# A selective scan and a routed feed-forward on one Trainium2 core: who makes the ten products du*B in the first half of each batch

## The reference, cut to what matters

```
delta = softplus(dt_proj @ dt_lo + bias)            # [b, e, t]
dA    = exp(delta * A[e, n])
state = state * dA + (delta * u)[e, t] * B[n, t]    # du*B: the product
y     = sum over n of state * C[n, t]
x     = x + transpose((y + D*u) * silu(layernorm(x)))
```

```
logits = layernorm(x).reshape(-1) @ switch_w.T + switch_b   # one routing per batch, top 2 of 8
h  = gelu(x_head @ w1[expert] + b1[expert])                 # 16 heads of 64
o  = sum over the two experts of gate * (h @ w2[expert] + b2[expert])
out = x + (layernorm(x) + o) @ w3.T + b3
```

## Time and profile before

| | |
|---|---|
| time, median of 3 | 2447.03 us |
| profiled execution | 2449.12 us, its span 2447.1 us |
| VectorE busy | 2121.5 us, 87% |
| TensorE busy | 1991.9 us, 81% |
| ScalarE busy | 1601.4 us, 65% |
| GpSimd busy | 1525.9 us, 62% |
| mean granted TensorE clock | 0.904 |

### The profile page before, as it was taken

The page is one execution under the profiler, slowest core; times in us unless marked ns, Lnnn a source line. Parts: engine busy times, 40 slices in busy tenths (PEclk is TensorE's granted clock), DMA queues, the critical chain, the costliest instruction groups (busy, mean ns, idle before and its releaser), DMA issues.

```text
span 2447.1 us, 32499 instructions
## 1 busy us (share of the span) xinstructions
PE 1991.9 (81%) x10584; PEld 1180.8 (48%) x10584; DVE 2121.5 (87%) x2694; ACT 1601.4 (65%) x2357; POOL 1525.9 (62%) x1061
## 2 busy tenths in 40 slices
PE   6898889986857987996757897898785787787899
PEld 2677667754533553443434454354453354344344
DVE  5899799979998999989999899998999899899311
ACT  2687877766668868655658977855666857854500
POOL 0698677767755765666766675576775577577111
PEclk9899999997878999997878998899786899899899
DMA  5311515555512944566621554466461174467512
GB/s 176 126 40 58 194 53 172 185 196 200 196 52 70 318 146 130 164 208 206 235 84 69 201 201 141 149 223 207 166 221 31 52 254 164 141 213 284 205 57 72
DMA packets 199290, 383.00 MB, mean 157 GB/s; under 512 B 30513, under 2 KB 96049, under 8 KB 199122
## 3 DMA queue, kind: packets, MB, share of 16 engines
q1 hardware_dynamic: 195952, 380.46, 46.2%
q10 hardware_dynamic: 3170, 0.47, 0.1%
HBM read 346.79 MB, written 34.08 MB: 156 GB/s over the span
## 4 chain that ended last, share of the span: by engine, by line
PE 32%; DVE 22%; issue 22%; ACT 16%; POOL 6%; DMA 1%; DVEq 1%; POOLq 0%; ACTq 0%; SPq 0%
DVE h L1547 10%; PE dense L1161 10%; PE dense L989 5%; POOL h L876 5%; ACT dA L1270 4%; DVE dense L1523 4%; PE dense L927 3%; ACT L1239 3%; PE dense L1086 2%; DVE u L1383 2%; PE dense L975 2%; PE dense L939 2%; PE dense L1144 2%; PE dense L996 2%; ACT hs L1357 2%
## 5 line engine op out<-in xcount | busy, mean ns | idle before, releaser
L876 POOL TENSOR_TENSOR h<-h,Cb 128x1024 f32<-128x1024 f32 x512 | 1208.3, 2361 | 375.0 <-DVE h L1547 349.1
L1270 ACT ACTIVATE dA<-delta,Av 128x512 f32<-128x512 f32 x1024 | 703.3, 716 | 390.9 <-DVE h L1547 387.9
L989 PE MATMUL dense<-ident,h 128*128 128x128 f32 x4096 | 601.6, 298 | 155.0 <-POOL h L876 154.3
L989 PEld LDWEIGHTS dense<-ident,h 128*128 128x128 f32 x4096 | 518.1, 155 | 309.7 <-POOL h L876 222.3
L1547 DVE TENSOR_TENSOR_SCAN h<-dA,state,dense 128x512 f32<-128x512 f32 x512 | 628.8, 1268 | 18.5 <-PE dense L989 7.6
L1547 DVE TENSOR_TENSOR_SCAN h<-dA,dense 128x512 f32<-128x512 f32 x512 | 597.2, 1205 | 12.9 <-PE dense L989 8.4
L1523 DVE TENSOR_TENSOR dense<-dense,Bb 128x512 f32<-128x512 f32 x864 | 552.4, 687 | 1.6
L1161 PE MATMUL dense<-w3h,xT 128*128 128x512 f32 x832 | 384.8, 598 | 1.3 <-DVE xT L1503 1.3
L870 POOL COPY state<-h 128x2 f32<-128x2 f32 x256 | 47.7, 186 | 319.3 <-DVE h L1547 317.6
L927 PE MATMUL dense<-ctxs,win 128*128 128x512 f32 x432 | 209.8, 631 | 10.2 <-ACT szT L1299 9.0
L1161 PEld LDWEIGHTS dense<-w3h,xT 128*128 128x128 f32 x832 | 148.3, 192 | 137.7 <-issue 135.8
(11 more groups left out here) (167 smaller groups left out, 2009.9 us busy)
## 6 DMA issues: line engine op xcount, KB each, us to landing
sww<-in_sw SPq DMA_DIRECT2D x167, 512.0 KB, 4.3
Cb<-bc_scratch SPq DMA_DIRECT2D x64, 512.0 KB, 6.6
Bb<-bc_scratch SPq DMA_DIRECT2D x54, 512.0 KB, 4.8
w3h<-in_sw SPq DMA_DIRECT2D x52, 512.0 KB, 8.0
w3h<-in_w3T SPq DMA_DIRECT2D x52, 512.0 KB, 5.2
row<-x_scratch SPq DMA_DIRECT2D x40, 512.0 KB, 4.8
xz<-in_x SPq DMA_DIRECT2D x64, 256.0 KB, 4.7
xt<-in_x SPq DMA_DIRECT2D x64, 256.0 KB, 4.1
```

The lines of the kernel that those rows point to most:

```text
L876: e.tensor_tensor(h[:, s:s + 2, :], h[:, s:s + 2, :], Cb[:, 2 * q:2 * q + 2, :], ALU.mult).then_inc(prod_done, 1)
L989: mm = e.matmul(yT[:, k, :], h[:, 2 * ((PAIRS * g + q) % RH) + i, k * P:(k + 1) * P], ident[:], is_transpose=True, start=False, stop=(q == ...
L1270: e.activation(dA[:, i % RA, :], delta[:, st % 2, :], ACT.Exp, scale=Av[:, j * N + n:j * N + n + 1]).then_inc(dA_done, 1)
```

## The change

TensorE makes the ten products in steps 0 to 7 of batches 1 to 3 too (`pe_step`: 24 more steps). With it:

- The product banks are laid out ahead by `ProductBanks`: F1, M0 and M1 in turn where TensorE makes products, M0 and M1 elsewhere, and the transposed du takes a turn in the same rotation instead of F0.
- F1 is therefore taken from the feed-forward in first halves: for `u=0` the second hidden half and the second tile bank are F2, `turn 0` uses F0 alone at its own, earlier slots, `turn 1` uses F1 and waits for the last scan of step 7; for `u=1` the tiles go F1, F0.
- `duT` has one buffer, copied in slot 7 behind the du copy. b3 gets half a buffer of its own (`b3half`), loaded four times a batch, each load waiting on SP for the addition before.
- The diagonals are no longer made from bank F2 by VectorE after batch 0's start: Bb is loaded for all pairs, and GpSimd masks it in place with `affine_select`, ten times at each of four chunk changes (into step 8 of batch 0 and step 0 of batches 1 to 3), four in the old chunk's last step and six in the new one's slots 0 to 3.

```diff
+HALF_PAIRS = PE_PAIRS
...
+def pe_step(g):
+    return g < STEPS or g % STEPS < J
...
 def on_pe(g, n):
-    return g < STEPS and n // 2 in PE_PAIRS
+    return pe_step(g) and n // 2 in (PE_PAIRS if g < STEPS else HALF_PAIRS)
-def product_bank(g, n):
-    return (F1, M0, M1)[(N * g + n) % 3] if g < STEPS else (M0, M1)[n % 2]
+class ProductBanks:
+    def __init__(self):
+        self.bank, self.before = {}, {}
+        order, held = [F1, M0, M1], {}
+        for g in range(ALL):
+            for n in range(N):
+                if n == N - 2 and g + 1 < ALL and pe_step(g + 1):
+                    self.place(order, held, ("turn", g + 1), order)
+                self.place(order, held, ("product", g, n), order if pe_step(g) else [k for k in order if k != F1])
...
+            for i in (0, 1):
+                t = ((11, 13), (17, 19), (24, 26), (27, 29))[k][i]
+                self.add(b, t, "turn", 0, k, i)
+                self.add(b, t + 1, "turned", 0, k, i)
...
+                self.add(b, at[W3C * (TB * dh - 1)] + 3 if dh else at[0] - 2, "b3_load", u, dh)
...
-            return [((what, *args), F0 + i if u == 0 or b == NB else F2)]
+            return [((what, *args), F0 + i if b == NB else F1 if u else F0)]
         if what == "hidden":
             first = M0 if b == NB and args[1] % 2 else F0
-            return [((what, *args, i), first + i) for i in (0, 1)]
+            second = F2 if b < NB and args[0] == 0 else first + 1
+            return [((what, *args, i), (first, second)[i]) for i in (0, 1)]
...
+            return [((what, *args[:3]), (F1, F0)[m % 2] if args[0] else (F0, F2)[m % 2])]
...
             def load_bc(c, q):
-                for i, dst in ((N, Cb),) if on_pe(J * c, 2 * q) else ((0, Bb), (N, Cb)):
+                for i, dst in ((N, Cb),) if c == 0 and on_pe(0, 2 * q) else ((0, Bb), (N, Cb)):
...
+            def diagonal_b(c, n):
+                e.wait_ge(bc_loaded[n // 2], bc_value(c, n // 2))
+                e.affine_select(out=Bb[:, n, :].rearrange("p (k t) -> p k t", k=TB), in_=Bb[:, n, :].rearrange("p (k t) -> p k t", k=TB),
+                                compare_op=ALU.is_equal, fill=0.0, base=0, pattern=[[0, TB], [-1, P]], channel_multiplier=1) \
+                    .then_inc(diag_done, 1)
...
+                    for n in range(N):
+                        at = n // 2 + 4 + n % 2
+                        if j == J - 1 and at == q and c + 1 < NB * TH and on_pe(g + 1, n):
+                            diagonal_b(c + 1, n)
+                        if j == 0 and at == SLOTS + q and c and on_pe(g, n):
+                            diagonal_b(c, n)
...
-                if b == 0:
-                    if q == 1 and j == J - 1 and g + 1 < STEPS:
-                        turn_b(c + 1, count(b, "x_proj", th) + 1)
-                    if q == 2:
-                        first_sum(g)
+                if b == 0 and q == 2:
+                    first_sum(g)
+                if b < NB:
                     times_b_at(N * g + 2 * q + 3)
-                    if q == SLOTS - 2 and g + 1 < STEPS:
-                        turn_du(g + 1)
+                    if q == SLOTS - 2 and g + 1 < ALL and pe_step(g + 1):
+                        if not pe_step(g):
+                            last = ("tile", 1, NQ - 1, TB - 2)
+                            e.wait_ge(evac[bank_of(b, *last)], 1 + count(b, *last) + 1)
+                        wait_product_bank(e, ("turn", g + 1))
+                        turn_du(g + 1, BANKS.bank[("turn", g + 1)])
...
                     if q == SLOTS - 1 and g + 1 < ALL:
                         copy_du(g + 1)
+                        if pe_step(g + 1):
+                            copy_duT(g + 1, BANKS.bank[("turn", g + 1)])
...
-                if j == J - 1 and g + 1 < STEPS and q and on_pe(g + 1, 2 * (q - 1)):
-                    for n in (2 * q - 2, 2 * q - 1):
-                        diagonal_b(c + 1, n)
```

More of the change, by code:

```diff
@@ L52, in conv_slot, with place @@
     return 2 if st % J == J - 1 else 1
+def pe_step(g):
+    return g < STEPS or g % STEPS < J
 def on_pe(g, n):
-    return g < STEPS and n // 2 in PE_PAIRS
-def product_bank(g, n):
-    return (F1, M0, M1)[(N * g + n) % 3] if g < STEPS else (M0, M1)[n % 2]
+    return pe_step(g) and n // 2 in (PE_PAIRS if g < STEPS else HALF_PAIRS)
[8 more added lines that the diff above has]
+                self.place(order, held, ("product", g, n), order if pe_step(g) else [k for k in order if k != F1])
+    def place(self, order, held, name, among):
+        k = among[0]
+        self.bank[name], self.before[name] = k, held.get(k)
+        held[k] = name
+        order.remove(k)
+        order.append(k)
+BANKS = ProductBanks()
 class Schedule:
@@ L222, in tail @@
         for dh in range(NQ):
+            self.add(b, 46, "b3_load", 0, dh)
+        for dh in range(NQ):
             for u in (0, 1):
@@ L320, in build @@
         du_s = sb("du_s", [P, T])
-        duT = sb("duT", [P, 2, TB, P])
+        duT = sb("duT", [P, TB, P])
+        b3half = sb("b3half", [P, QD])
         h = sb("h", [P, 2 * RH, T])
@@ L500, in chunk_block, with turns_of_du, diag_index, wait_product_bank @@
             return G // STEPS, G // J % TH, G % J
+        made = [0]
+        for g_ in range(ALL):
+            made.append(made[-1] + sum(on_pe(g_, m) for m in range(N)))
         def pe_index(g, n):
-            return 2 * len(PE_PAIRS) * min(g, STEPS) + sum(on_pe(g, m) for m in range(n))
+            return made[g] + (sum(on_pe(g, m) for m in range(n)) if g < ALL else 0)
         def vec_index(g, n):
             return N * g + n - pe_index(g, n)
-        def bank_free(g, n):
-            return N * g + n - (2 if g < STEPS else 1)
-        def bc_value(c, q):
-            return 1 + sum(16 if on_pe(J * i, 2 * q) else 32 for i in range(c + 1))
+        def turns_of_du(g):
+            return sum(pe_step(i) for i in range(g))
+        def diag_index(c, n):
+            return sum(on_pe(J * i, m) for i in range(c) for m in range(N)) + sum(on_pe(J * c, m) for m in range(n))
+        def wait_product_bank(e, name):
+            before = BANKS.before[name]
+            if before and before[0] == "product":
+                e.wait_ge(h_done, 1 + N * before[1] + before[2] + 1)
+            elif before:
+                e.wait_ge(duT_done, 1 + turns_of_du(before[1]) + 1)
+        def bc_value(c, q):
+            return 1 + 32 * (c + 1) - (16 if on_pe(0, 2 * q) else 0)
+        def b3_of(b, uu, dh):
+            if b == NB:
+                return (duT[:].rearrange("p k t -> p (k t)") if dh else b3half[:]), 1 + 16 * (2 * NQ * (NB - 1) + dh + 1)
+            return b3half[:], 1 + 16 * (2 * NQ * (b - 1) + NQ * uu + dh + 1)
         def f_index(b, k):
```

73 lines of the change are left out of this document (34 added, 39 removed).

## The result

The changed kernel takes 2469.59 us (median; 2464.88 to 2471.55) where the kernel before, in the same measurement, takes 2446.81 (2446.35 to 2447.78). The ratio is 1.0088, with a 95% interval of 1.0073 to 1.0103. The prediction said 2408.4 us, faster by 1.6%. It is wrong in sign, and the time lies outside its range.

What follows compares the result with a forecast made beforehand. VectorE was taken to bound steps 0 to 4, VectorE and TensorE step 7. Batches 1 to 3 at -11.4, -10.4 and -15.8, with batch 0, sum to -38.6 us: from 2447.0 to 2408.4, range 2370 to 2440.

Steps and rivals of the forecast that it cites:

- Batch 0's plain steps, which run the way the change wants: Batch 0 steps with products already on TensorE, 25.2 us each, taken as a model for the new steps.
- What leaves VectorE: Ten products a step, 5.9 us, over 24 steps: 142 us, the ceiling of the gain.
- Steps 0, 2 and 3: Batch 1 scan steps, predicted at 29.5 us (-2.8), 29.8 us (-4.8) and 31.7 us (+0.2).
- Step 1: Batch 1 scan step, predicted at 27.2 us (-5.1).
- Step 4: Batch 1 step with routing on VectorE and TensorE nearly idle, predicted at 35.0 us (-5.5).
- Steps 5 and 6: Steps paced by ScalarE's gelu and table loads: a gain of 1.5 us each in batch 1, 1 in the others.
- slower by the coupling of the heads: Steps 5, 6: hidden matmul waits for scan; 2.6 us a pair, 2478 us, 7%; milder 1.0 us, 2439 us, 10%.
- Step 7: Step with TensorE already full: 42.5 us (+9.6) in batches 1 and 2, +4.2 in batch 3.
- The mask: GpSimd's 128x512 masks at chunk changes, taken at 1.0 us each, six of them in step 0.
- The clock: TensorE's granted clock in steps 0 to 3 of batches 1 to 3: near 1, as in batch 0.
- The rival that the clock stays low: Steps 0 to 3 keep their clock of 0.62 to 0.89: +40.6 us in all, 2488 us; chance 3%.
- Layout, b3 loads, batch 0, second halves: Bank turns and b3 loads 0 (10 us kept for the range), batch 0 -1 us, steps 8 to 15 unchanged.

Runs made afterwards that it cites:

- experiment 1: Changed kernel with first_sum issued ahead of product 7 in the 24 new steps, not behind product 8: 2437.07 us, ratio 0.9950.
- experiment 2: Changed kernel with first_sum issued behind product 8 in batch 0 too: 2503.48 us, ratio 1.0218.
- experiment 4: The kernel of experiment 1 with the hidden matmuls of the 24 new steps also issued ahead of product 2q+3: 2411.00 us, ratio 0.9843.
- experiment 5: Changed kernel with the hidden matmuls issued ahead of product 2q+3, first_sum left behind product 8: 2439.93 us, ratio 0.9956.
- experiment 3: Changed kernel with HALF_PAIRS = (): VectorE makes all products of batches 1 to 3, new layout kept: 2445.98 us, ratio 0.9979.
- experiment 9: The kernel of experiment 4 with eight products a step, HALF_PAIRS = (1, 2, 4, 6), pair 5 given back to VectorE: 2397.02 us, ratio 0.9787.

## Why the prediction was wrong, step by step

**The step that failed** is the basis of all: "Batch 0's plain steps, which run the way the change wants". I took the rows of batch 0 as the model for the new halves, and summed loads over it. They don't run that way: the code places `first_sum` by batch, and this was in the lines I had read. The prediction priced the loads of each engine and the clock, but never listed TensorE's queue in a slot of a later batch, item by item, with whom each item waits for and who waits behind it. So its sum has no term for such a wait in steps 0 to 3, 0.4 us in step 4, and a gain in steps 5 and 6. Experiments 1 and 2 show this one place: 34 us when it is mended, 34 us when it is brought into batch 0 (458.0 us there in the change, 492.4 in experiment 2). Only slot 2's order changed in them. The 17.5 us by which a half came out over the forecast (mean of three) are step 4 with 8.2, step 1 with 4.7, steps 5 and 6 with 6.3 and step 2 with 1.9, less 3.1 in step 7 and 0.4 in steps 0 and 3.

- *What leaves VectorE*: right. 130.8 us of busy time in the halves, for 142 predicted.
- *Steps 0, 2 and 3*: 29.4, 31.7 and 31.0 for 29.5, 29.8 and 31.7. Step 0 is right by luck: it holds 2.6 us of idle time before scan 6 that the prediction didn't have, and masks much shorter than it took; in experiment 1, without that idle time, it is 27.4 (mean). *Step 1*: 32.6 for 27.2, the largest error of the plain steps, and of it 3.70 us are the gap shown above. Experiment 1 has 28.8 there (mean of the three batches).
- *Step 4*: 43.2 for 35.0, the largest error. The 5.5 us of gain were counted in full because TensorE was "nearly idle". More than half of the error is the late first sum: scan 6 waits 3.70 us in this step too, and experiment 1 has it at 38.8 (mean). A second wait follows where routing ends, in the timeline of the changed kernel:

```profile
690.62 4.67 DVE L1619 TENSOR_TENSOR_SCAN h<-dA,dense 128x512 f32<-128x512 f32 x4
...
691.98 2.05 PE L1046 MATMUL dense<-Bb,duT 128*128 128x128 f32 x8 [10.04 <-DVE h L1619]
...
694.68 1.91 PE L1046 MATMUL dense<-Bb,duT 128*128 128x128 f32 x8
...
696.38 1.85 PE L1060 MATMUL dense<-ident,h 128*128 128x128 f32 x8
...
698.37 2.33 DVE L1619 TENSOR_TENSOR_SCAN h<-dA,dense 128x512 f32<-128x512 f32 x2 [3.08 <-PE dense L1060]
```

  Routing holds the scans back, so no product bank comes free, and TensorE stands still for 10.04 us. The granted clock is 0.76 over the step; a product takes 2.05 us behind that stretch where it takes 1.13 in step 5, and scan 12 waits 3.08 us for a sum that stands behind two products. Experiment 4 leaves step 4 at 38.3 (mean), still 3.3 over the prediction. There too TensorE stands idle ahead of the product (7.73 us), and scan 12 waits behind it, but for 1.52 us:

```profile
681.44 2.05 PE L1046 MATMUL dense<-Bb,duT 128*128 128x128 f32 x8 [7.73 <-DVE h L1622]
...
686.26 2.33 DVE L1622 TENSOR_TENSOR_SCAN h<-dA,dense 128x512 f32<-128x512 f32 x2 [1.52 <-PE dense L1060]
```

  So this wait can account for about half of what is left; what holds the rest is open. With eight products the step is 37.9.
- *Steps 5 and 6*: 40.0 and 43.2 for 38.0 and 40.3. The mechanism was described ("each slot of TensorE begins by waiting for that slot's first scan"), given as bounds, and then valued at a gain of 1.5 us a step in batch 1 and 1 in the others. Against before, the two steps took 3.9 us a half more (means 40.0 and 43.2 for 38.6 and 40.7), 0.5 us for each of the eight pairs of heads: inside the bounds of -1.5 to +2.6, with the sign of the rival "slower by the coupling of the heads", which I had at 10% in its milder form and 7% in the full one. Moving the hidden matmul ahead gives 26 us (experiment 4 against 1) to 32 us (experiment 5 against the change). Either order mended alone makes the kernel faster than before (0.9950 and 0.9956), so the loss took both.
- *Step 7*: longer and with TensorE busy throughout (38.77 of 39.10 us at clock 1.00), as predicted, and mis-sized: 39.1 for 42.5, in batch 3 35.0 for 37.4. The 40.0 us of added-up work was closer than the 42.7 that I got by dividing by a share of busy time of 0.935; measured, the share is 0.99. That the load alone sets this length is likely for ten products (two fewer take 1.1 us off) and not so for eight (two fewer again take off nothing).
- *The mask*: 0.639 us for the 1.0 taken, so six in step 0 are 3.8 us and not 6, from the groups of GpSimd in the changed kernel:

```profile
L912 POOL TENSOR_SCALAR_AFFINE_SELECT Bb<-Bb 128x512 f32<-128x512 f32 x40 | 24.9, 639 | 0.0
```

- *The clock*: right in steps 0 to 3. Steps 0 to 3 of batch 1 went from 0.68, 0.79, 0.75 and 0.89 to 0.94, 0.90, 1.00 and 1.00. The rival that the clock stays low falls. Of the rule that stood behind it (the Trainium skill, "TensorE: Matmul & The Clock Gate", section "A second HAM failure mode: psum-queue depth-cycling", which tells it of one bf16 kernel with 512 columns) the trace shows the opposite here: with products cycling through three banks the clock rose. TensorE was idle for 12.0 us of step 0 before and for 4.9 after.
- *Layout, b3 loads, batch 0, second halves*: 0 predicted, and 0 by experiment 3 and the sums above.

With the order mended at both places (experiment 4) the halves of the profiled execution give 44.3 us, where the same terms of the prediction summed to 37.6, and 0.9843 x 2447.0 is 2408.6 us, where 2408.4 was predicted. That is a forecast for another kernel than the one I was given, and it agrees by luck: in the means of the three batches steps 4 and 1 were put 3.3 and 1.6 us too low, and steps 7, 5 and 0 3.3, 2.3 and 2.1 too high. The two positions in the queue make 60 us between them (1.0088 against 0.9843), about the whole distance of 61 us between forecast and result.

## What to carry to other kernels

When work moves onto an in-order engine, write out that engine's queue around it, item by item: what each waits for, and what stands behind it that another engine needs. A new item that waits for X's latest result must not stand ahead of an item that X's next step needs. Loads and rows of a stage "that already does it" prove nothing about another stage until both queues have been compared line by line, and the right order of the new mixture can be the wrong one of the old. After an engine's work has been moved, look for the balance again: here eight products a step beat both ten and six, and which eight mattered too (experiment 9). A share of busy time near 1 is no proof of a bound; taking work off is.

## What the runs showed of the hardware

- `affine_select` on 128x512 takes 0.639 us on GpSimd, 2.2 times the 128x128 one (0.292) and half of a two-input operation of that size (1.275). The scans of VectorE that ran beside a mask for over 0.3 us, 24 in all, were no slower than those beside none: 1202 and 1259 ns in the mean against 1206 and 1264 (without and with `state` among their inputs).
- A ring between two engines also shows as a lower clock. With the sum late, batch 0's plain steps have 0.92 in place of 1.00 with the same TensorE instructions, and their TensorE busy time for five steps grew from 115.70 to 124.98 us. A low granted clock can thus follow from a wait.
- After TensorE had been idle for 10.04 us, its next three groups of eight took 2.05, 1.91 and 1.85 us; from 698 on they took 1.06 and 1.04.
- The second halves of batches 1 to 3, in which VectorE makes all products in every kernel here, sum to between 861 and 871 us in single profiles (to the end of the last scan): some of their steps vary (step 15 of batches 1 and 2: 43.9 to 46.1). Differences of some 10 us between the sums of two single profiles can come from this alone.
